# Router passes and Gelu's table moved among the last batches; up-products issued before the preceding down-products in the feed-forward stage

## Chip, cores and metric

One core of one Trainium2 chip runs the whole kernel. The metric is the device time of one execution in microseconds (us). Three executions of the kernel before took 1644.10, 1644.18 and 1648.24 us.

## The reference

16 sequences of 512 tokens with 128 features pass one layer. Cut to what matters for the change:

```python
h = take(W.T, x)                                     # 16 x 512 x 128
h = h + low_rank_attention(layernorm(h), W1, W2)     # one softmax over 512 keys
x = layernorm(h)
pooled = x.mean(axis=1)                              # 16 x 128
g = gelu(pooled @ router_w1.T + router_b1)
route = softmax(g @ router_w2.T + router_b2)         # 16 x 8
idx_s, idx_t = argmax(route[:, :4]), argmax(route[:, 4:])
fused = three_attentions(layernorm(x), idx_s, idx_t) # experts' weights by idx
x = x + fused
h2 = layernorm(x) * norm_mlp_w + norm_mlp_b
x = x + gelu(h2 @ mlp_w1.T + b1) @ mlp_w2.T + b2     # 128 -> 512 -> 128
out = h + x
```

The router (five lines from `pooled` on) needs the means of all 16 sequences. Its result says which experts' weights the attentions load.

## The kernel before

Three functions run one after the other, each in a block of its own. A block ends when every engine has come to the end of its program for it; the next one starts then. In a block each engine has its own program, in order, and semaphores join them. The helper `halves_of_pairs` calls a body for each batch number b, with the first pairs and the last ones written out and a hardware loop between them. A body handles several batches at different stages: `exists(b - 3)` is false where that batch is outside 0 to 15.

**embed_and_mix** gathers the tokens and does the first attention. Its second half has one step for each b:

- PE (`mix_and_turn`): the logits of b+1 (L620), the product of probabilities and X of b (`mix`, L632), then `turn` of b-3: 4 tokens' groups times a column of 1/512 into column b of a PSUM bank (L642, the pooling, 8 matmuls in the profile), and then the transposes of the twice normalised batch xh (L648). The two parts of `turn` stand in this order, and the first waits for `x_ready`, the second for `xh_ready`.
- ACT (`soften_and_keep`): Exp of b+1's logits (L526), `keep` of b-3 (L531 copies xs to X; L533 copies the transposed batch from PSUM to xhatT, after the transposes), `again` of b-2 (L541 writes xh, after DVE's `shift`).
- DVE (`second_norms`): the division and residual of b into h (L428, L432), its statistics, the shift of b-2 (L442), and normalise and statistics of b-1 (L356, L346, L351). POOL computes the reciprocal roots (L328, L332).

After the last step stands the router: DVE copies the pooled columns (L462), PE multiplies with router_w1 (L669), ACT applies Gelu (L556), PE multiplies with router_w2 (L671), DVE adds the bias and finds the maximum, ACT applies Exp with a sum (L558), DVE finishes softmax and argmax (L470 to L486), and SyncE stores the 32 numbers into the tile `expert` (L295). ACT keeps its functions in table sets. Where the program has no load of its own, the compiler sets one before the first function that needs another set: so before Gelu (L556), before the Exp behind it (L558) and in the block after (L1200).

**attend** is the long stage, 1270 us of the span. SyncE reads `expert` in it and loads w_in_S by it. The change leaves its code as it is.

**feed_forward** has one step for each b in each engine:

- PE (`stages`): `turn` of b (4 transposes, L1513; waits for `normed` and `hT_ready`), `down` of b-3 (32 matmuls in the profile, L1528; waits for the four Gelus of that batch), `up` of b-2 (8 matmuls, L1520; waits for hT, and for each quarter until the Gelu of the batch before it has read the PSUM bank).
- ACT (`gelu`): four Gelus for each batch (L1500), each as soon as its quarter of `up` is there. The tile gT has two halves, so Gelu of b waits until `down` of b-2 is done.
- DVE (`stages`): normalise of b (L1459), statistics of b+1, scale_shift of b-1 (hT, L1473; waits for `up` of b-3 to have read the tile's other use), `finish` of b-3 (y, L1467; waits for `down`, for POOL's base and for the store of y two batches back).
- POOL (`sequence`): the root of b, then base of b-4 (L1434, L1437), which waits for `finish` of the batch before, since `base` is one tile.
- SyncE fetches h of b+2 after base_a of b and stores y of b.

PE's step:

```python
if exists(b):
    turn(b, odd)
if exists(b - 3):
    down(b - 3, 1 - odd)
if exists(b - 2):
    up(b - 2, odd)
```

The batches' numbers in what follows are those of the argument, so turn(15) is the last batch's.

Of the kernel before, what the change touches and what calls it, by code (L numbers as in the profile page):

```python
# [6 lines left out]
ACT = mybir.ActivationFunctionType  # L7
# [7 lines left out]
B, T = 16, 512  # L15
NB = T // P
H, HD = 8, 16
K = 4
# [149 lines left out]
def tokens(tile, b, n):  # L168

    return tile[:, bass.ds(NB * b + n, 1), 0:P].rearrange("p o d -> p (o d)")  # L170


def embed_and_mix(nc, shared, x_ids, table, w12, router_w1, router_b1, router_w2, router_b2, norms, out_v):

    scrap, ident, low, high, eps_t, minus_half, norm_cols, expert, X, xhatT, psum = shared
    with ExitStack() as ctx:
# [91 lines left out]
        with nc.Block() as block:  # L268
# [74 lines left out]
            def _(dve):  # L343
# [79 lines left out]
                def second_norms(b, odd):  # L423

                    if exists(b):
                        dve.wait_ge(summed, b + 1)
                        sums = psum[:, 4:6, :].rearrange("p a (c e) -> p a c e", c=2)
                        nc.vector.reciprocal(rsum[:].rearrange("p (a c) -> p a c", a=2), sums[:, :, :, P])\  # L428
                            .then_inc(recip, 1)
                        dve.wait_ge(recip, b + 1)  # L430
                        for n in range(NB):
                            last = nc.vector.scalar_tensor_tensor(  # L432
                                out=tokens(h, b, n), in0=sums[:, n // 2, n % 2, 0:P], scalar=rsum[:, n:n + 1],
                                in1=tokens(h, b, n), op0=ALU.mult, op1=ALU.add)
                        last.then_inc(h2_ready, 1)
                        dve.wait_ge(h2_ready, b + 1)
                        settle(nc, scrap)
                        statistics(lambda n: tokens(h, b, n), b, six2, stats2, mv2[:, odd, :, :])
                    if exists(b - 2):
                        dve.wait_ge(rstd3, b - 1)  # L440
                        at_least(dve, xh_ready, b - 2)
                        nc.vector.scalar_tensor_tensor(out=shift3[:], in0=mv3[:, :, 0], scalar=-1.0, in1=rstd3_t[:],  # L442
                                                       op0=ALU.mult, op1=ALU.mult).then_inc(shift_ready, 1)
# [14 lines left out]
                halves_of_pairs(dve, second_norms, 2, B // 2, B // 2 + 1)  # L458


                dve.wait_ge(pooled_in, B)
                nc.vector.tensor_copy(pooled[:], psum[:, POOLED, 0:B]).then_inc(r_dve, 1)  # L462
                dve.wait_ge(r_pe, 2)
                nc.vector.tensor_tensor(rl[:], psum[0:B, 1, 0:2 * K], rb2[:], ALU.add).then_inc(r_dve, 1)
                dve.wait_ge(r_dve, 2)
# [23 lines left out]
            def _(act):  # L489
# [55 lines left out]
                def soften_and_keep(b, odd):  # L545
                    if exists(b + 1):
                        soften(b + 1, 1 - odd)
                    if exists(b - 3):
                        keep(b - 3, 1 - odd)
                    if exists(b - 2):  # L550
                        again(b - 2, odd)

                soften(0, 0)
                halves_of_pairs(act, soften_and_keep, 2, B // 2 - 1, B // 2 + 2)
                act.wait_ge(r_pe, 1)
                nc.scalar.activation(rh[:], psum[:, 0, 0:B], ACT.Gelu, bias=rb1[:]).then_inc(r_act, 1)  # L556
                act.wait_ge(r_dve, 4)
                nc.scalar.activation(rex[:], rl[:], ACT.Exp, bias=rsc[:, 1:2], accum_out=rsc[:, 2:3]).then_inc(r_act, 1)  # L558

            @block.tensor  # L560
            def _(pe):
# [74 lines left out]
                                start=(s == 0), stop=(s == NB - 1))  # L636
                    last.then_inc(summed, 1)

                def turn(b, odd):
                    pe.wait_ge(x_ready, b + 1)  # L640
                    for n in range(NB):
                        last = nc.tensor.matmul(psum[:, POOLED, bass.ds(b, 1)], xs[:, odd, n, :], mean_col[:],  # L642
                                                start=(n == 0), stop=(n == NB - 1))
                    last.then_inc(pooled_in, 1)
                    pe.wait_ge(xh_ready, b + 1)
                    at_least(pe, xhatT_kept, b)
                    for n in range(NB):
                        last = nc.tensor.transpose(psum[:, TURN, P * n:P * n + P], xh[:, n, :], ident[:])  # L648
                    last.then_inc(turned2, 1)

                def mix_and_turn(b, odd):
# [3 lines left out]
                        logits(b + 1)  # L655
                    if exists(b):
                        mix(b, odd)
                    if exists(b - 3):
                        turn(b - 3, 1 - odd)

                pe.wait_ge(rows_in[0], 16 * NPART)
                pe.wait_ge(x_kept[0], 8 * B)
# [1 line left out]
                pe.wait_ge(reduced, 2 * B)  # L664
                logits(0)
                halves_of_pairs(pe, mix_and_turn, 3, B // 2 - 1, B // 2 + 2)
                pe.wait_ge(r_dve, 1)
                pe.wait_ge(exped, B)
                nc.tensor.matmul(psum[:, 0, 0:B], rw1[:], pooled[:], start=True, stop=True).then_inc(r_pe, 1)  # L669
                pe.wait_ge(r_act, 1)  # L670
                nc.tensor.matmul(psum[0:B, 1, 0:2 * K], rh[:], rw2[:], start=True, stop=True).then_inc(r_pe, 1)  # L671


def attend(nc, shared, s_in, s_out, t_in, t_out, c_in, c_out, c_bias):
# [679 lines left out]
def feed_forward(nc, shared, mlp_w1, mlp_b1, mlp_w2, mlp_b2, out_v):  # L1354

    scrap, ident, low, high, eps_t, minus_half, norm_cols, expert, X, xhatT, psum = shared
    with ExitStack() as ctx:
# [31 lines left out]
        with nc.Block() as block:  # L1389
# [53 lines left out]
            def _(dve):  # L1443
# [32 lines left out]
                def stages(b, odd):  # L1476
# [3 lines left out]
                        statistics(b + 1)  # L1480
                    if exists(b - 1):
                        scale_shift(b - 1, 1 - odd)
                    if exists(b - 3):
                        finish(b - 3, 1 - odd)

                statistics(0)
                halves_of_pairs(dve, stages, 3, B // 2 - 1, B // 2 + 2)
# [18 lines left out]
            def _(pe):  # L1506
# [25 lines left out]
                def stages(b, odd):  # L1532
                    if exists(b):
                        turn(b, odd)
                    if exists(b - 3):
                        down(b - 3, 1 - odd)
                    if exists(b - 2):
                        up(b - 2, odd)

                halves_of_pairs(pe, stages, 3, B // 2, B // 2 + 2)  # L1540

# [59 lines left out]
```

## Time and profile before

| | |
|---|---|
| three executions | 1644.10, 1644.18, 1648.24 us (median 1644.18) |
| the profiled execution's own time | 1643.73 us |
| its span, first to last instruction | 1642.0 us |
| mean granted TensorE clock | 0.950 |
| PE busy | 1513.5 us, 92% of the span |
| DVE, ACT, POOL busy | 1221.4, 1129.2, 998.9 us |
| second half of embed_and_mix with the router | from 106.1 to 222.5 us |
| attend | from 222.5 to 1495.0 us |
| feed_forward | from 1495.0 us to the end |

The profile is of one execution. Times in it are microseconds from the first instruction, and 1643.73 - 1642.0 = 1.7 us lie around the span. A row of the timeline gives start, duration, engine, line, operation, tiles and count, and in square brackets how long the engine sat idle ahead of it and what ended that. PEld is TensorE's load of weights, which overlaps its matmuls. The ends of matmuls are modelled, so their starts are the better numbers. The granted clock is 1.00 at 2.4 GHz and 0.50 at 1.2 GHz.

### The profile page before, as it was taken

The numbers are of one execution on the slowest core, as the hardware profiler recorded it, in microseconds if no ns is written. First come the engines' busy times: TensorE is split into PE (matmuls) and PEld (weight loads), VectorE is DVE, ScalarE is ACT, GpSimd is POOL, SyncE is SP. The second block draws the span as 40 slices with busy tenths as digits, with TensorE's granted clock in tenths as the row PEclk, the third lists the DMA queues.
The fourth block names the chain that finished last, engine by engine and source line by source line (L and its number), as shares of the span: only waits on it lengthen the run. The fifth ranks groups of instructions, "written<-read, shape, count | busy, mean of one in ns | idle before, by whom it ended". The sixth has DMA issues, their size and how long they took to land. (4 is left out here: it accounts for less than half of the span.)

```text
span 1642.0 us, 37445 instructions
## 1 busy us (share of the span) xinstructions
PE 1513.5 (92%) x8694; PEld 662.1 (40%) x8694; DVE 1221.4 (74%) x3412; ACT 1129.2 (69%) x2201; POOL 998.9 (61%) x1359
## 2 busy tenths in 40 slices
PE   5779949899999999999999999999999999885998
PEld 1238823233333433333333333333333333212665
DVE  6868848489888887978888887978888897253442
ACT  5757733567887878787787878778787878723332
POOL 7704443756777776766777686776777684513443
PEclk9779957999999999999999999999999999957999
DMA  3311143644554654654564564564565552111221
GB/s 83 103 31 46 52 74 50 83 77 71 79 84 62 81 77 62 85 74 72 74 85 62 73 84 63 78 79 73 67 88 65 68 79 44 25 15 34 66 69 53
DMA packets 140020, 110.34 MB, mean 67 GB/s; under 512 B 22720, under 2 KB 134464, under 8 KB 139968
## 3 DMA queue, kind: packets, MB, share of 16 engines
q1 hardware_dynamic: 137920, 105.53, 43.4%
q0 software_dynamic: 2048, 4.20, 1.1%
q8 instruction: 23, 0.38, 0.1%
q14 instruction: 29, 0.24, 0.1%
HBM read 19.29 MB, written 8.39 MB: 17 GB/s over the span
## 5 line engine op out<-in xcount | busy, mean ns | idle before, releaser
L1153 ACT ACTIVATE probs<-psum 128x512 f32<-128x512 f32 (+3 forms) x1536 | 755.0, 548 | 225.7 <-PE psum L1268 215.0
L1053 DVE TENSOR_REDUCE mx_S<-psum 128x1 f32<-128x512 f32 x512 | 326.3, 681 | 48.6 <-PE psum L1248 47.6
L1053 DVE TENSOR_REDUCE mx_C<-psum 128x1 f32<-128x512 f32 x512 | 317.8, 676 | 45.3 <-PE psum L1248 45.3
L1049 DVE CUSTOM_DVE_ANT_0 psum<-psum,causal 128x128 f32<-128x128 f32 (+3 forms) x512 | 242.5, 509 | 98.1 <-PE psum L1248 95.5
L1248 PE MATMUL psum<-ks_S,qs_S 96*128 96x512 bf16 x512 | 197.6, 397 | 10.4 <-DMA ks_S<-parts_k 6.3
L1248 PE MATMUL psum<-ks_C,qs_C 96*128 96x512 bf16 x512 | 199.6, 398 | 4.6 <-DMA ks_C<-parts_k 1.4
L1268 PE MATMUL psum<-qs_C,ks_C 99*128 99x512 bf16 x512 | 189.3, 385 | 3.6 <-ACT probs L1153 3.2
L1268 PE MATMUL psum<-qs_S,ks_S 99*128 99x512 bf16 x512 | 190.5, 383 | 0.2
L934 POOL CAST parts_q<-f_q 128x512 bf16<-128x512 f32 x48 | 29.3, 610 | 226.7 <-ACT f_q L1144 226.2
L1248 PE MATMUL psum<-ks_T,qs_T 96*128 96x128 bf16 (+3 forms) x512 | 155.6, 306 | 1.6 <-DVE mx_S L1053 1.1
L1268 PE MATMUL psum<-qs_T,ks_T 99*128 99x256 bf16 (+3 forms) x512 | 152.1, 301 | 3.0 <-ACT probs L1153 1.7
L1287 PE MATMUL psum<-probs,va_S 128*32 128x512 f32 x1024 | 136.4, 604 | 1.6 <-ACT u_all L1173 0.3
L1287 PE MATMUL psum<-probs,va_C 128*32 128x512 f32 x1024 | 137.0, 607 | 0.8 <-ACT u_all L1173 0.6
L1248 PEld LDWEIGHTS psum<-ks_C,qs_C 96*128 96x128 bf16 x512 | 49.8, 97 | 166.8 <-DVE mx_C L1053 124.3
L922 POOL TENSOR_SCALAR_AFFINE_SELECT probs<-probs 128x512 f32<-128x512 f32 x128 | 81.0, 634 | 56.7 <-ACT probs L1153 53.7
L1248 PEld LDWEIGHTS psum<-ks_S,qs_S 96*128 96x128 bf16 x512 | 50.3, 99 | 153.9 <-DVE mx_S L1053 104.1
L1500 ACT ACTIVATE gT<-psum,b 128x512 f32<-128x512 f32 x64 | 44.0, 687 | 94.3 <-PE psum L1520 94.3
L1248 PEld LDWEIGHTS psum<-ks_T,qs_T 96*128 96x128 bf16 x512 | 50.1, 98 | 135.0 <-DVE mx_T L1049 91.2
L1287 PE MATMUL psum<-probs,va_T 128*32 128x512 f32 (+3 forms) x1024 | 96.3, 448 | 3.5 <-POOL probs L922 2.4
L988 POOL TENSOR_TENSOR s_all<-s_all,s_high 128x512 f32<-128x512 f32 x48 | 60.9, 1269 | 23.5 <-ACT u_high L1163 23.5
L316 POOL DMA_INDIRECT h<-in_table,ids x64 | 60.6, 947 | 20.4 <-issue 19.2
L1268 PEld LDWEIGHTS psum<-qs_C,ks_C 99*128 99x128 bf16 x512 | 49.4, 98 | 58.2 <-ACT probs L1153 23.9
(186 smaller groups left out, 2705.8 us busy)
## 6 DMA issues: line engine op xcount, KB each, us to landing
qs_S<-parts_q SPq DMA_DIRECT2D x96, 128.0 KB, 4.5
ks_S<-parts_k SPq DMA_DIRECT2D x96, 128.0 KB, 5.0
qs_T<-parts_q SPq DMA_DIRECT2D x96, 128.0 KB, 4.4
ks_T<-parts_k SPq DMA_DIRECT2D x96, 128.0 KB, 4.6
qs_C<-parts_q SPq DMA_DIRECT2D x96, 128.0 KB, 4.4
ks_C<-parts_k SPq DMA_DIRECT2D x96, 128.0 KB, 4.9
w_in_S<-in_s_in SPq DMA_DIRECT2D x16, 257.0 KB, 2.8
w_in_T<-in_t_in SPq DMA_DIRECT2D x16, 257.0 KB, 2.7
```

The source lines that it names most:

```text
L316: nc.gpsimd.indirect_dma_start(h[:, NB * b + n, :], None, table, bass.IndirectOffsetOnAxis(ap=ids[:, NB * b + n:NB * b + n + 1].bitcast(U3 ...
L922: nc.gpsimd.affine_select(out=diagonal, in_=diagonal, compare_op=ALU.is_ge, fill=0.0, base=0, pattern=[[0, 4], [1, P]], channel_multiplier ...
L934: nc.gpsimd.tensor_copy(parts[c][:, 0, :], f32[c][:]).then_inc(hi_done, 1)
L988: nc.gpsimd.tensor_tensor(s_all[:], s_all[:], s_high[:], ALU.add).then_inc(s_merged, 1)
L1049: nc.vector.tensor_tensor_reduce(tile[:, 0:last_key], tile[:, 0:last_key], causal[:, T - last_key:T], 1.0, NEG, ALU.add, ALU.max, mx[kind] ...
L1053: nc.vector.tensor_reduce(mx[kind][:, n:n + 1], tile, AX_X, ALU.max, negate=True).then_inc(reduced, 1)
L1153: nc.scalar.activation(probs[:, group_place(kind, b, n // 4), n % 4, t0:T], psum[:, LOGITS + ring_place(kind, b, n, RC), t0:T], ACT.Exp, s ...
L1248: nc.tensor.matmul(psum[:, ring_place(kind, b, n, RL), 0:keys], qs[kind][0:RA, hd, P * tb:P * tb + P], ks[kind][0:RA, hd, 0:keys], start=T ...
L1268: nc.tensor.matmul(psum[:, bank, t0:T], ks[kind][0:RB, hd, P * s:P * s + P], qs[kind][0:RB, hd, t0:T], start=True, stop=True).then_inc(log ...
L1287: last = nc.tensor.matmul(sums[32 * j:32 * j + 32, t0:T], va[kind][:, s, g, j, :], probs[:, group_place(kind, b, q), j, t0:T], start=(s == 0),
L1500: nc.scalar.activation(gT[:, odd, f, :], psum[:, 1 + f, :], ACT.Gelu, bias=b1[:, f:f + 1])\
```

## The change

In embed_and_mix:

- PE: the pooling is cut out of `turn` and called for b-2 ahead of `turn` of b-3. The router's two matmuls move from behind the last step into the last one with work (b = 18), between mix and turn(15).
- ACT: an explicit load of Gelu's table set stands in step 16, ahead of keep(13) and again(14). The router's Gelu and Exp stand in step 17 between keep(14) and again(15).
- DVE: the copy of the pooled columns moves into step 17, ahead of the shift of batch 15.

In feed_forward PE issues up of b-2 ahead of down of b-3, and DVE's `finish` comes one step later (b-4 in place of b-3).

```diff
@@ second_norms (DVE) @@
+                    if isinstance(b, int) and b == B + 1:
+                        dve.wait_ge(pooled_in, B)
+                        nc.vector.tensor_copy(pooled[:], psum[:, POOLED, 0:B]).then_inc(r_dve, 1)
                     if exists(b - 2):
                         dve.wait_ge(rstd3, b - 1)
...
-                dve.wait_ge(pooled_in, B)
-                nc.vector.tensor_copy(pooled[:], psum[:, POOLED, 0:B]).then_inc(r_dve, 1)
                 dve.wait_ge(r_pe, 2)
@@ soften_and_keep (ACT) @@
                     if exists(b + 1):
                         soften(b + 1, 1 - odd)
+                    if isinstance(b, int) and b == B:
+                        nc.scalar.add_instruction(mybir.InstLoadActFuncSet(
+                            name=nc.get_next_instruction_name(), engine=mybir.EngineType.Activation, ins=[], outs=[],
+                            act_func_set_id=GELU_SET))
                     if exists(b - 3):
                         keep(b - 3, 1 - odd)
+                    if isinstance(b, int) and b == B + 1:
+                        route()
                     if exists(b - 2):
                         again(b - 2, odd)
 
+                def route():
+                    act.wait_ge(r_pe, 1)
+                    nc.scalar.activation(rh[:], psum[:, 0, 0:B], ACT.Gelu, bias=rb1[:]).then_inc(r_act, 1)
+                    act.wait_ge(r_dve, 4)
+                    nc.scalar.activation(rex[:], rl[:], ACT.Exp, bias=rsc[:, 1:2], accum_out=rsc[:, 2:3]).then_inc(r_act, 1)
+
                 soften(0, 0)
                 halves_of_pairs(act, soften_and_keep, 2, B // 2 - 1, B // 2 + 2)
-                act.wait_ge(r_pe, 1)
-                nc.scalar.activation(rh[:], psum[:, 0, 0:B], ACT.Gelu, bias=rb1[:]).then_inc(r_act, 1)
-                act.wait_ge(r_dve, 4)
-                nc.scalar.activation(rex[:], rl[:], ACT.Exp, bias=rsc[:, 1:2], accum_out=rsc[:, 2:3]).then_inc(r_act, 1)
@@ PE @@
-                def turn(b, odd):
+                def pool_tokens(b, odd):
                     pe.wait_ge(x_ready, b + 1)
                     for n in range(NB):
                         last = nc.tensor.matmul(psum[:, POOLED, bass.ds(b, 1)], xs[:, odd, n, :], mean_col[:],
                                                 start=(n == 0), stop=(n == NB - 1))
                     last.then_inc(pooled_in, 1)
+
+                def turn(b, odd):
                     pe.wait_ge(xh_ready, b + 1)
...
                         mix(b, odd)
+                    if exists(b - 2):
+                        pool_tokens(b - 2, odd)
+                    if isinstance(b, int) and b == B + 2:
+                        route()
                     if exists(b - 3):
                         turn(b - 3, 1 - odd)
+
+                def route():
+                    pe.wait_ge(r_dve, 1)
+                    pe.wait_ge(exped, B)
+                    nc.tensor.matmul(psum[:, 0, 0:B], rw1[:], pooled[:], start=True, stop=True).then_inc(r_pe, 1)
+                    pe.wait_ge(r_act, 1)
+                    nc.tensor.matmul(psum[0:B, 1, 0:2 * K], rh[:], rw2[:], start=True, stop=True).then_inc(r_pe, 1)
...
-                pe.wait_ge(r_dve, 1)
-                pe.wait_ge(exped, B)
-                nc.tensor.matmul(psum[:, 0, 0:B], rw1[:], pooled[:], start=True, stop=True).then_inc(r_pe, 1)
-                pe.wait_ge(r_act, 1)
-                nc.tensor.matmul(psum[0:B, 1, 0:2 * K], rh[:], rw2[:], start=True, stop=True).then_inc(r_pe, 1)
@@ feed_forward, stages (DVE) @@
-                    if exists(b - 3):
-                        finish(b - 3, 1 - odd)
+                    if exists(b - 4):
+                        finish(b - 4, odd)
@@ feed_forward, stages (PE) @@
                         turn(b, odd)
+                    if exists(b - 2):
+                        up(b - 2, odd)
                     if exists(b - 3):
                         down(b - 3, 1 - odd)
-                    if exists(b - 2):
-                        up(b - 2, odd)
```

## Rows read from the trace of the kernel before

**Rows 1.** The page, part 4: shares of the span in the chain that ended last
```profile
PE psum L1528 4%; PE psum L1520 3%; ACT gT L1500 1%; DVE xs L1459 0%; PE psum L1513 0%; DVE y L1467 0%; DVE hT L1473 0%; DVE mv L1451 0%
```

**Rows 2.** Waits of PE, 1498 to 1642: total us, times, longest us
```profile
PE psum L1528 <- ACT gT L1500: 6.8, 15, 0.8
```

**Rows 3.** Timeline of the feed-forward stage, PE: one step in full
```profile
1513.49 3.84 PE L1528 MATMUL psum<-w,gT 128*128 128x128 f32 x32 [0.34 <-ACT gT L1500]
...
1517.17 3.60 PE L1520 MATMUL psum<-hT,w 128*128 128x512 f32 x8
...
1520.60 0.60 PE L1513 MATMUL psum<-ident,xs 128*128 128x128 f32 x4
...
1521.54 3.84 PE L1528 MATMUL psum<-w,gT 128*128 128x128 f32 x32 [0.34 <-ACT gT L1500]
```

**Rows 4.** Timeline of the feed-forward stage's last steps
```profile
1606.90 3.10 DVE L1459 TENSOR_SCALAR xs<-X,mv,rstd_t 128x128 f32<-128x128 f32 x4
...
1610.05 0.66 PE L1513 MATMUL psum<-ident,xs 128*128 128x128 f32 x4 [0.36 <-DVE xs L1459]
1610.54 3.77 PE L1528 MATMUL psum<-w,gT 128*128 128x128 f32 x32
1614.14 3.60 PE L1520 MATMUL psum<-hT,w 128*128 128x512 f32 x8
...
1618.52 3.84 PE L1528 MATMUL psum<-w,gT 128*128 128x128 f32 x32 [0.78 <-ACT gT L1500]
...
1630.45 0.69 DVE L1467 TENSOR_TENSOR y<-base,psum 128x512 f32<-128x512 f32 x1 [7.37 <-PE psum L1528]
...
1632.54 1.27 POOL L1437 TENSOR_TENSOR base<-base,b 128x512 f32<-128x512 f32 x1
```

**Rows 5.** Timeline of the end of embed_and_mix and of the router
```profile
208.22 1.11 DVE L356 TENSOR_SCALAR xs<-h,mv,rstd_t 128x128 f32<-128x128 f32 x4
208.23 1.65 ACT L541 ACTIVATE xh<-xs,shift,rstd 128x128 f32<-128x128 f32 x4 [0.92 <-DVE shift L442]
...
210.62 1.83 PEld L642 LDWEIGHTS psum<-mean_col,xs 128*128 128x128 f32 x8
...
212.25 1.65 ACT L541 ACTIVATE xh<-xs,shift,rstd 128x128 f32<-128x128 f32 x4 [0.57 <-DVE shift L442]
...
213.95 1.12 PE L648 MATMUL psum<-ident,xh 128*128 128x128 f32 x4 [1.40 <-ACT xh L541]
214.64 0.55 PEld L669 LDWEIGHTS psum<-pooled,rw 128*128 128x128 f32 x2
...
215.10 0.60 ACT L533 ACTIVATE xhatT<-psum 128x512 f32<-128x512 f32 x1 [0.69 <-PE psum L648]
215.72 1.28 ACT L556 ACT_TABLE_LOAD   x1
217.01 0.27 ACT L556 ACTIVATE rh<-psum,rb 128x16 f32<-128x16 f32 x1
...
218.80 0.18 ACT L558 ACTIVATION_READ_ACCUMULATOR rex<-rl,rsc 16x1 f32 x1
...
220.39 0.53 SPq L295 DMA_DIRECT2D expert<-rid_i  x1
222.52 1.28 ACT L1200 ACT_TABLE_LOAD   x1 [3.54 <-PEq L268]
```

**Rows 6.** Timeline at the end of attend and the block boundary behind it
```profile
1493.99 0.69 DVE L1120 TENSOR_TENSOR X<-X,psum 128x512 f32<-128x512 f32 x1 [4.98 <-PE psum L1304]
...
1494.97 1.28 ACT L1491 ACT_TABLE_LOAD   x1 [5.29 <-PEq L837]
```

**Rows 7.** Timeline of embed_and_mix, PE: mix(3), and a pooling in the loop
```profile
129.19 3.81 PE L632 MATMUL psum<-X,probs 128*128 128x129 f32 x32 [0.66 <-DVE h L432]
...
144.29 0.95 PE L642 MATMUL psum<-mean_col,xs 128*128 128x1 f32 x8
```

**Rows 8.** Busy time by stretch: us, PE, PEld, DVE, ACT, POOL, PEclk, DMA share, GB/s
```profile
275.00:309.00 34.00, 29.59 (x183) 9.88 (x181) 12.23 (x50) 28.47 (x60) 19.74 (x28) 1.00 0.41 56
```

## The prediction

> **What bounds the kernel now.** I read the page's chain of waits first. It ends in the feed-forward stage and goes through the down-products, the up-products and Gelu there [rows 1]. So that stage is bound by PE and by one wait on ACT. The waits of PE in the stage show it: 15 times PE sits idle ahead of the down-products until a Gelu is done, 6.8 us in all [rows 2]. The timeline of one step shows why. PE runs down, up, turn; the up-products' last quarter ends as turn begins, its Gelu ends after turn, and only then may the next down start [rows 3]. The up-products are thus directly ahead of the Gelu that the next down needs. In the last three steps there is no turn between them, and the idle time is 0.78 us instead of 0.34 [rows 4].
>
> The other edited place is the end of embed_and_mix. The timeline there is a serial chain: normalise, pooling, transposes, copy, table load, Gelu, Exp, the store of the experts' numbers, and then the next block [rows 5]. Nothing in that stretch has a bound; every engine waits most of the time. Attention between the two places has no edited code.
>
> **The feed-forward stage.** Nothing is added or removed; the order changes. The cost of a step, by starts, since the ends are modelled: down to up is 1517.17 - 1513.49 = 3.68 us; up to turn is 1520.60 - 1517.17 = 3.43 us; turn to down was 0.94 us [rows 3]. Without a wait for Gelu, turn to the next matmul takes 1610.54 - 1610.05 = 0.49 us: the one step in which turn itself came late shows that [rows 4]. A free step is 3.68 + 3.43 + 0.49 = 7.60 us. From the first down, 1513.49, to the thirteenth, 1610.54, there are 12 steps in 97.05 us [rows 3, 4], 8.09 us each. So a step with a turn loses 0.49 us, and there are 13: 6.4 us. The three steps without a turn: 1618.52 - 1614.14 = 4.38 us from up to down [rows 4] where 3.43 would do, 0.95 us each, 2.85 us in all. Sum 9.2 us.
>
> Does anything take the wait's place? With up of b-2 ahead of down of b-3, the down's Gelus were fed by the up-products of the step before, so they have a whole down of slack, 3.68 us. Gelu of b-2 needs down of b-4, which ends just ahead of this step's turn: no wait. The transposes need DVE's normalise. DVE now finishes b-4 at the start of PE's step b and normalises b+1 behind it (0.69 + 1.11 us), needed 7.6 us later; before, only up's 3.43 us lay between. That also covers the one slow normalise, 3.10 us at 1606.90 where others take 1.11, which made PE wait 0.36 us [rows 4, 5]. The queue of POOL: base of a batch waits for the finish of the batch before. At the very end down(15) now follows down(14) at once, in 3.7 to 3.8 us. From finish to the end of base it took 1632.54 + 1.27 - 1630.45 = 3.36 us [rows 4]. It fits with 0.4 us to spare; if it didn't, the excess would be late once. SyncE fetches h behind the same base and keeps a full step. Cost of all this: zero, with 1 us as the upper end, since PE's loop branches were covered by the wait for Gelu and could show. The lower end of the gain is the idle time alone, 6.8 + 0.36 = 7.2 us less that 1 us, 6.2; I take 9.2, because starts are recorded and ends are not.
>
> **The end of embed_and_mix.** Step by step, against the rows of before [rows 5].
> - Pooling one step earlier in the steady loop: the same work in each PE step. It needs x_ready, which DVE gives while PE is still in mix. In step 2 a pooling is now there that wasn't: 0.95 us against 0.66 us that PE then waited for DVE's h [rows 7]. It costs 0 to 0.3 us; I take 0, for starts in the loop put a pooling at 0.8 us and the idle time is short by as much.
> - The table load in step 16, 1.28 us, meets ACT's 0.92 us of idle time ahead of again(14). So again(14) starts at most 0.36 us late, 208.6, and ends at 210.2. It is hidden, since PE has the pooling to do first.
> - pool(15) no longer stands behind turn(14). x_ready comes at 208.22 + 1.11 = 209.33 and it loads from 209.4 in place of 210.62; at 1.8 us it is done at 211.2.
> - turn(14) follows at 211.2. From turn to the copy was 215.10 - 213.95 = 1.15 us, so xhatT of 14 is copied from 212.35 to 212.95. The router's first product loads 0.7 us after turn's start and takes 0.55 plus 0.1: 212.6.
> - Gelu follows the copy at once, 212.97, where it was at 217.01: 4.04 us sooner. What went: one batch's turn and copy, and 1.28 us of load.
> - From Gelu's start to the store of the experts' numbers was 220.39 - 217.01 = 3.38 us, and to the next block 5.51 us. By that branch alone the block would end at 218.5. Exp's own table load of 1.28 us stays in it.
> - The added wait: again(15) is queued behind Exp on ACT, and turn(15) and keep(15) behind it. Exp's sum is there 218.98 - 217.01 = 1.97 us after Gelu's start: again(15) at 214.95 instead of 212.25. From its start to the end of the last copy was 215.70 - 212.25 = 3.45 us, so ACT ends at 218.4.
> - The boundary of blocks: 0.3 us from the last instruction to the next block at the other boundary [rows 6], 2.1 us here from the store's issue, its landing included [rows 5]. I take 0.4, nearest to the first, since ACT's copy has no DMA behind it: 218.8. That is 222.5 - 218.8 = 3.7 us sooner, with 2.0 and 4.1 as the ends.
>
> ACT's load shows no drain: it lasts 1.28 us and Gelu starts 0.01 us behind it [rows 5]. The Trainium skill (ScalarE: Activation LUTs, What ACT_TABLE_LOAD costs) puts a drain of about 1.38 us on top of every load. By it the early load would push again(14) back by that much more; it is the third rival. The trace speaks against it.
>
> **The sum.** The profiled execution took 1643.73 us, 0.45 us under the median of 1644.18. 1643.73 - 9.2 - 3.7 = 1630.8 us, 0.8% less. A measurement of this kernel can tell about 0.3%, 5 us, from no change.
>
> **The rivals.**
> 1. *The feed-forward stage does not get faster* (6%). PE would find another wait in front of turn or up, as long as Gelu's was. For it: the stage has a single base tile and two halves of most others, and `finish` is one step later. Against: each slack worked out above is over 2 us, but for the last batch. Then 1643.73 - 3.7 = 1640.0.
> 2. *The router's branch gains nothing* (6%). That is so if the chain behind again(15) takes 3.7 us longer than worked out, or if the compiler sets its own loads around the explicit one, two more at 1.28 us each. For it: two chains end within 0.4 us of each other, so none has spare. Against: Copy and Identity run without a load behind Exp's set, and a load for Gelu of the program's own stands in front of the feed-forward stage without a second one. Then 1643.73 - 9.2 = 1634.5.
> 3. *Loads cost their drain* (2%). again(14) then starts 1.4 us later at 210.0, ends at 211.6, turn(14) and Gelu slip by 0.4, and another 1.4 us lies ahead of Exp and so of again(15): the block ends at 220.6. The time is 1643.73 - 9.2 - 1.9 = 1632.6. The page named above is where that drain stands.
> 4. *Slower: attention starts on a lower clock* (5%). The granted clock was 1.00 from 275 to 309, and PE was busy for 29.6 of these 34 us [rows 8]. Attention now begins 3.7 us earlier with regard to whatever sets the level, behind a stretch in which PE does little. If the whole of that stretch fell to 0.50, its matmuls would take up to 29.6 us more. This decides the sign from 12.9 us of matmul time at the lower level on. All of it gives 1660; two thirds give 1650, which I name as its time. For it: the level changed several times before 344 us, and three runs of one kernel spread over 4.1 us. Against: those runs have the same kind of start and differ by 4 us only. The Trainium skill (TensorE: Matmul & The Clock Gate, What's actually happening) says that the window in which activity is judged is free-running and does not begin with the kernel; the spread of the runs agrees with that and doesn't prove it.
>
> The forecast itself, both parts by these mechanisms, has the rest, 81%.
>
> **How the numbers follow.** The time is the forecast's, 1630.8. The ends of the known costs: feed-forward gains 6.2 to 9.5 us, the router 2.0 to 4.1, together 1630.1 to 1635.5. The clock moves it by some 4 us up as between the three runs and, as the start may also be luckier, as much down: 1626.1 to 1639.5. That takes in rivals 2 and 3 and leaves out rival 4 and rival 1, which are 11%. I keep 1626 to 1639. Faster by over 0.3% is under 1639.2: the forecast, rivals 2 and 3, 89%. Within 0.3% is rival 1 with a bit of the clock, 6%. Slower is rival 4, 5%.
>
> **What would show it.** In the changed profile: down-products start 7.6 us apart with no wait for Gelu ahead of them, and 7.1 us in the last steps; the waits of PE in the stage hold nothing for L1500's Gelu of note; down(15) directly follows down(14). In the router: one table load ahead of keep(13), none directly at Gelu, Gelu near 213.0, again(15) behind Exp near 215, the next block near 218.8, and ACT's last copy the later of the two ends. Wrong would be: idle time ahead of turn or up of 0.3 us or more in each step, a wait of DVE for POOL's base at the end, a second load in step 16 or 17, or a start of attention later than 220. The clock rival would show as longer matmuls between 222 and 344 at 0.50, with everything else as said.

## The result and the profile after

The changed kernel took 1628.04 us, the median of five executions (1627.90 to 1629.27). The kernel before, timed between them, took 1644.75 us (1644.10 to 1648.24). The ratio is 0.9899, with a 95% interval of 0.9885 to 0.9912. So the change made the kernel faster by 1.0%, 16.7 us by the medians. The forecast was 1630.8 us, in a range of 1626 to 1639.

The profiled execution took 1629.0 us and its span is 1627.2 us. Against before's 1643.73 and 1642.0 that is 14.7 and 14.8 us less. By stages, from one block's first table load to the next:

| | before | after | gained |
|---|---|---|---|
| up to the block behind the router | 222.52 us | 218.30 us | 4.2 us |
| attend | 1272.45 us | 1273.38 us | -0.9 us |
| feed_forward, table load to the last y's start | 143.53 us | 132.11 us | 11.4 us |

Of the first 4.2 us, 0.1 us lies ahead of the second half of embed_and_mix: its table load of Exp starts at 100.56 us before and at 100.44 us after. The last y of the kernel before, and in the changed kernel the table load that opens the last stage, POOL's last base and the last y (timelines):

```profile
1638.50 0.69 DVE L1467 TENSOR_TENSOR y<-base,psum 128x512 f32<-128x512 f32 x1 [7.37 <-PE psum L1528]
```

```profile
1491.68 1.28 ACT L1508 ACT_TABLE_LOAD   x1 [5.29 <-PEq L854]
...
1622.31 1.27 POOL L1454 TENSOR_TENSOR base<-base,b 128x512 f32<-128x512 f32 x1
1623.79 0.69 DVE L1484 TENSOR_TENSOR y<-base,psum 128x512 f32<-128x512 f32 x1 [2.89 <-PE psum L1545]
```

The page of the changed kernel, part 4, the chain that ended last:

```profile
PE psum L1545 4%; PE psum L1537 3%; PE psum L1530 0%; DVE xs L1476 0%; DVE hT L1490 0%; DVE y L1484 0%; DVE mv L1468 0%
```

Gelu, 1% of the chain before [rows 1], is no longer in it. Line numbers have moved by 17: the down-products are L1545, the up-products L1537, the transposes L1530. The busy time between the first and the last down-products of the changed kernel (columns: length, then busy us of PE, PEld, DVE, ACT, POOL, granted clock, DMA share, GB/s):

```profile
1513.00:1623.00 110.00, 110.00 (x668) 83.11 (x667) 65.03 (x169) 39.32 (x58) 50.54 (x52) 1.00 0.23 67
```

PE is busy for all of the 110 us. Its waits for a Gelu, 6.8 us in 15 times before [rows 2], are gone. The timeline of PE in the same kernel, one step and the last ones, answers to [rows 3, 4]:

```profile
1513.11 3.73 PE L1545 MATMUL psum<-w,gT 128*128 128x128 f32 x32
1516.68 0.60 PE L1530 MATMUL psum<-ident,xs 128*128 128x128 f32 x4
1517.12 3.60 PE L1537 MATMUL psum<-hT,w 128*128 128x512 f32 x8
1520.55 3.73 PE L1545 MATMUL psum<-w,gT 128*128 128x128 f32 x32
...
1609.43 3.73 PE L1545 MATMUL psum<-w,gT 128*128 128x128 f32 x32
...
1616.44 7.31 PE L1545 MATMUL psum<-w,gT 128*128 128x128 f32 x64
```

A step is 1520.55 - 1513.11 = 7.44 us, where 8.09 us was the mean before and 7.60 us the forecast. A last step, one without a turn, is 1616.44 - 1609.43 = 7.01 us. The last two down-products are one row of 64 matmuls: nothing lies between them.

The end of embed_and_mix in the changed kernel, from the timeline (answers to [rows 5]):

```profile
205.96 1.28 ACT L550 ACT_TABLE_LOAD   x1
...
207.25 0.63 ACT L532 ACTIVATE X<-xs 128x512 f32<-128x512 f32 x1
...
211.08 1.09 PE L659 MATMUL psum<-ident,xh 128*128 128x128 f32 x4
211.26 0.17 DVE L441 COPY pooled<-psum 128x16 f32<-128x16 f32 x1 [0.63 <-PE psum L651]
...
212.22 0.60 ACT L534 ACTIVATE xhatT<-psum 128x512 f32<-128x512 f32 x1 [1.79 <-PE psum L659]
212.71 0.27 ACT L562 ACTIVATE rh<-psum,rb 128x16 f32<-128x16 f32 x1
213.00 1.28 ACT L564 ACT_TABLE_LOAD   x1
...
214.59 1.63 ACT L542 ACTIVATE xh<-xs,shift,rstd 128x128 f32<-128x128 f32 x4
...
216.08 0.53 SPq L295 DMA_DIRECT2D expert<-rid_i  x1
...
217.43 0.60 ACT L534 ACTIVATE xhatT<-psum 128x512 f32<-128x512 f32 x1 [0.69 <-PE psum L659]
218.30 1.28 ACT L1217 ACT_TABLE_LOAD   x1 [0.28 <-PEq L268]
```

Every step stands in the order that was worked out. There is one load of Gelu's set, at 205.96, and the copy behind it starts 0.01 us after its end. Gelu runs at 212.71 instead of 217.01. again(15), at 214.59, now stands behind Exp, and ACT's last copy ends at 218.03. The next block begins 0.3 us later. The store of the experts' numbers, issued at 216.08, had 2.22 us by then; before, the block began 2.13 us after its issue. So the two branches end almost together: by before's 2.13 us the store alone would let the block begin at 218.21, 0.1 us sooner than it did. (The load that opens the block, L1217 here and L1200 before, is the program's own and not the compiler's.)

### The profile page after: what moved, and what is told of

Read it like the earlier page. It is cut to its first block and busy times, and to the rows that moved or that the text cites. A ratio compares the mean times of both kernels' runs of the same rounds, so it can differ in the third digit from the quotient of the medians.

```text
span 1627.2 us, 37445 instructions
## 1 busy us (share of the span) xinstructions
PE 1510.4 (93%) x8694; PEld 661.2 (41%) x8694; DVE 1241.3 (76%) x3412; ACT 1129.1 (69%) x2201; POOL 1000.1 (61%) x1359
```

## The experiments

These ran on three other chips of the same kind, on which the kernel before takes 1704 to 1705 us. The surplus lies in the first stage: the load of Exp's table ahead of the second half starts at 159.35 us in the changed kernel on the third of them and at 100.44 us on the chip above. From there on its stages last as long as here: 118.0 us to the next block (117.9 here), 1273.5 us of attention (1273.4), and 132.1 us of feed-forward (132.1). Each kernel is compared with the kernel before on its own chip, and stages are compared by traces. Times on the timeline in the expectations are those of the first chip, so some 59 us have to be added.

**The two parts alone.** The first kernel has embed_and_mix of the changed kernel and feed_forward of before, the second the other way round.

> The edits of embed_and_mix alone, feed_forward as before. Theory A (the two parts do not touch each other): the block after the router starts at 218.3 us as in the changed kernel, the stage of feed_forward lasts 144.2 us from its table load to its last y as before, and the time is 4.2 us under the kernel before, give or take 1 us in attention. Theory B (the shift of attention's start against the clock levels made part of the gain): attention lasts more than 2 us less or more than before's 1272.5 us, and the time is off by as much.

> The edits of feed_forward alone, embed_and_mix as before. Theory A (the two parts add): the stage lasts 132.8 us in place of 144.2, down-products start 7.44 us apart, and the time is 11.4 us under the kernel before. Theory of the prediction as it stood: 9.2 us, with 7.60 us from down to down.

The router's part alone: 1700.32 us against 1703.85, ratio 0.9978 (0.9968 to 0.9987), 3.5 us less. The feed-forward part alone: 1693.07 us, ratio 0.9944 (0.9928 to 0.9960), 10.8 us less. The changed kernel itself was timed again on a third chip:

> The changed kernel itself, timed on the same chip as the kernel with up ahead of turn. It serves as the mark for that kernel: the stage of feed_forward should last 131.8 us from its table load to its last down-product's start, and the time be 15 to 17 us under the kernel before.

1687.82 us against 1703.83, ratio 0.9904 (0.9887 to 0.9920), 16.0 us less; 3.5 + 10.8 = 14.3 us is within the runs' spread of that. In the traces the feed-forward stage shows the parts cleanly. The first fence is the timeline of the router's part alone, the second that of the feed-forward part alone (in each the table load that opens the stage, and the last y).

```profile
1554.02 1.28 ACT L1508 ACT_TABLE_LOAD   x1 [5.29 <-PEq L854]
...
1698.23 0.69 DVE L1484 TENSOR_TENSOR y<-base,psum 128x512 f32<-128x512 f32 x1 [7.37 <-PE psum L1545]
```

```profile
1554.09 1.28 ACT L1491 ACT_TABLE_LOAD   x1 [5.31 <-PEq L837]
...
1686.33 0.69 DVE L1467 TENSOR_TENSOR y<-base,psum 128x512 f32<-128x512 f32 x1 [2.88 <-PE psum L1528]
```

144.2 us and 132.2 us, with 7.44 us from down to down in the second (starts at 1590.54 and 1597.98); the whole change has 132.1 us. The first is 0.7 us longer than the 143.5 us of before; the expectations' 144.2 and 132.8 us counted to the end of the last y, and by that measure these are 144.9 and 132.9 us. The 0.7 us lie in the first up-products: 5.79 us to the transposes behind them instead of 5.13, at a granted clock of 0.59 instead of 0.66. At the end of embed_and_mix, Gelu's table load to the next block is 12.35 us in the router's part alone and 12.34 us in the changed kernel. So theory A holds for the two edited stages.

Theory B, of attention, is not excluded. Its mark was met in the first kernel: attention lasts 1275.95 us there, 3.5 us more than the 1272.45 us of before. The router's part as such does not bring that much, for the changed kernel has the same embed_and_mix and 1273.4 and 1273.5 us in two traces. But in the nine traces with the router moved attention lasts 1270.6 to 1276.0 us, 0.7 us more on average than in the four with the router in its old place, 1272.2 to 1272.5 us. The section on the prediction comes back to it.

**Why a step is 7.44 and not 7.60 us.** In the kernel before, down waits for three of the four Gelus and takes the third quarter twice in place of the fourth, so it leaves out a part of the result. PE's order is that of before.

```diff
-                    pe.wait_ge(gelu_done, F // P * b + F // P)
+                    pe.wait_ge(gelu_done, F // P * b + F // P - 1)
...
-                            last = nc.tensor.matmul(psum[:, DOWN[odd], P * n:P * n + P], gT[:, odd, f, P * n:P * n + P],
+                            last = nc.tensor.matmul(psum[:, DOWN[odd], P * n:P * n + P], gT[:, odd, min(f, 2), P * n:P * n + P],
```

> The kernel before, where down waits for three of its four Gelus and multiplies the third quarter of gT twice in place of the fourth (PE's work is the same in size; the fourth Gelu runs and nobody reads it). PE's order is that of before. Theory A (the loss of before was the wait for Gelu and, with it, the first load of weights, which a waiting matmul cannot have ahead of time: 0.11 us at down and 0.05 at turn): steps with a turn are 7.44 us apart, as in the changed kernel, and only the last three keep a short wait of 0.1 us or less; the stage lasts 133 to 134 us and the time is 10 to 11 us under the kernel before. Theory B (the order itself is cheaper, down to turn than down to up): 7.60 us a step, and 8 to 9 us under the kernel before.

1692.69 us against 1703.85, ratio 0.9934 (0.9919 to 0.9950), 11.2 us less. The timeline of PE in that kernel:

```profile
1580.95 3.74 PE L1528 MATMUL psum<-w,gT 128*128 128x128 f32 x32
1584.53 3.60 PE L1520 MATMUL psum<-hT,w 128*128 128x512 f32 x8
1587.96 0.60 PE L1513 MATMUL psum<-ident,xs 128*128 128x128 f32 x4
1588.40 3.74 PE L1528 MATMUL psum<-w,gT 128*128 128x128 f32 x32
```

Down, up, turn as before, and 7.45 us a step: theory A. In the steps of the loop the order is worth nothing by itself; the wait was all of it. The whole stage is 133.3 us to the last y's start, 1.1 us longer than with the changed order on the same chip: PE still waits 0.36 us for the one late normalise (of 3.10 us), and the last steps take 7.19 us instead of 7.01. And the wait cost more than its idle time: a step of 8.05 us, 0.34 us of it idle, became one of 7.44. Weight loads (PEld) show what. First the kernel before, the load and the matmul of a down that waited, then the changed kernel, where the first load runs ahead of its matmul and 31 are left in the row behind:

```profile
1618.52 3.65 PEld L1528 LDWEIGHTS psum<-w,gT 128*128 128x128 f32 x32 [1.61 <-ACT gT L1500]
```

```profile
1520.12 0.19 PEld L1545 LDWEIGHTS psum<-w,gT 128*128 128x128 f32 x1 [0.24 <-issue]
1520.55 3.54 PEld L1545 LDWEIGHTS psum<-w,gT 128*128 128x128 f32 x31 [0.24 <-issue]
```

Before, the load started with its matmul, at 1618.52 [rows 4]. Now it is done 0.24 us before the matmul starts, under the up-products. Down to the next kind takes 3.57 us instead of 3.68, and turn to the next 0.44 instead of 0.49. That it is the load that costs this is read from these rows; no run changed the load alone.

**The Gelu table.** The changed kernel without the explicit load.

```diff
-                    if isinstance(b, int) and b == B:
-                        nc.scalar.add_instruction(mybir.InstLoadActFuncSet(
-                            name=nc.get_next_instruction_name(), engine=mybir.EngineType.Activation, ins=[], outs=[],
-                            act_func_set_id=GELU_SET))
```

> The changed kernel without the explicit load of Gelu's table set in step 16; the compiler then sets one directly ahead of Gelu. Theory A (ACT's chain of Gelu, Exp, again(15) and keep(15) ends the block): Gelu starts at 214.0 instead of 212.7 and the next block at 219.6 instead of 218.3, 1.3 us later. Theory B (something else ends the block, and ACT has spare time): the next block starts less than 0.5 us later.

1688.26 us against 1704.96, ratio 0.9903 (0.9887 to 0.9920). In time that can't be told from the changed kernel (0.9904). The timeline of this kernel can tell it:

```profile
270.75 0.17 DVE L441 COPY pooled<-psum 128x16 f32<-128x16 f32 x1 [0.63 <-PE psum L647]
...
272.32 1.28 ACT L558 ACT_TABLE_LOAD   x1
273.62 0.27 ACT L558 ACTIVATE rh<-psum,rb 128x16 f32<-128x16 f32 x1
...
279.21 1.28 ACT L1213 ACT_TABLE_LOAD   x1 [0.28 <-PEq L268]
```

From the pooled copy to the next block it takes 279.21 - 270.75 = 8.46 us. In the changed kernel it is 218.30 - 211.26 = 7.04 us. The early load is worth 1.4 us of the router's 4.2, and of the two theories A holds: what hangs on ACT's Gelu ends the block. It does not tell ACT's own end from the store of the experts' numbers, for both moved with Gelu. The store is issued 2.22 us ahead of the next block here too, and ACT's last copy ends 0.27 us ahead of it. That ACT's is the later end, by some 0.1 us, rests on the 2.13 us of before.

**The pooling alone.** The kernel before, with the pooling moved ahead as in the change and nothing else.

```diff
+                    if exists(b - 2):
+                        pool_tokens(b - 2, odd)
                     if exists(b - 3):
                         turn(b - 3, 1 - odd)
```

> The kernel before, with the pooling of b-2 ahead of turn of b-3 and nothing else: the router stays behind the last step and its table loads stay where they were. Theory A (the gain comes from the router's place on ACT and PE, and the early pooling only allows it): the pooled copy comes some 1.3 us sooner, Gelu and the next block come when they did, within 0.2 us, and the time is that of the kernel before. Theory B (the pooling was on the chain): 1.3 us sooner.

1703.85 us in a single execution; the median of before on that chip is 1703.83. From its timeline:

```profile
271.91 0.17 DVE L462 COPY pooled<-psum 128x16 f32<-128x16 f32 x1
...
272.51 1.63 ACT L541 ACTIVATE xh<-xs,shift,rstd 128x128 f32<-128x128 f32 x4
...
282.77 1.28 ACT L1204 ACT_TABLE_LOAD   x1 [3.53 <-PEq L268]
```

From again(15) to the next block it is 10.26 us, and 222.52 - 212.25 = 10.27 us before [rows 5]. The pooled copy is 10.86 us ahead of the block instead of 9.94, 0.9 us sooner rather than 1.3, since in DVE's program it still stands behind the shift of batch 15, and nobody uses it. Theory A holds: the early pooling only makes room for the router's place.

**The slow normalise.** In the changed kernel DVE's normalise takes 3.06 to 3.10 us for the last eleven of the 16 batches and 2.35 us for the one ahead of them, where it took 1.11 us before and 3.10 us once [rows 4]. Its timeline:

```profile
1583.87 0.69 DVE L1484 TENSOR_TENSOR y<-base,psum 128x512 f32<-128x512 f32 x1 [1.72 <-PE psum L1545]
...
1584.47 3.07 DVE L1476 TENSOR_SCALAR xs<-X,mv,rstd_t 128x128 f32<-128x128 f32 x4
...
1584.81 1.30 POOL L1451 TENSOR_TENSOR base<-h,X 128x512 f32<-128x512 f32 x1 [1.98 <-DVE y L1484]
```

Both wait for the same y: POOL's base starts beside the normalise. The experiment cuts POOL's two adds to one column of each token group, with base set to zero once.

```diff
-                        nc.gpsimd.tensor_tensor(base[:], h2[:, odd, :, :], X[:, bass.ds(NB * c, NB), 0:P], ALU.add)\
+                        nc.gpsimd.tensor_tensor(base[:, :, 0:1], h2[:, odd, :, 0:1], X[:, bass.ds(NB * c, NB), 0:1], ALU.add)\
```

> The changed kernel, where POOL adds one column of each token group into base in place of 128 (the rest of base is set to zero once), so that its two adds are near 0.2 us each in place of 1.3. Theory A (DVE's normalise takes 3.07 us in place of 1.11 because POOL's adds of base run beside it): it takes 1.1 us in all steps, and the stage is as long as in the changed kernel, 132.8 us, since PE waits for neither. Theory B (the long normalise comes from something in DVE's own program, like the loop's branch or the fetch of code): it stays at 3.07 us.

From the timeline of that kernel:

```profile
1583.45 1.11 DVE L1479 TENSOR_SCALAR xs<-X,mv,rstd_t 128x128 f32 x4
1583.79 0.32 POOL L1454 TENSOR_TENSOR base<-h,X 128x4 f32<-128x4 f32 x1 [4.11 <-DVE y L1487]
```

1.11 us in every step, so theory A holds. The one slow normalise of before fits it: POOL's base starts at 1607.12 there, beside it, and beside none of the others. The step stays at 7.44 us and the stage at 132.2 us: PE does not wait for either. The single execution took 1687.53 us.

**The later finish.** The changed kernel with DVE's finish left at b-3, and the same with POOL's adds cut.

```diff
-                    if exists(b - 4):
-                        finish(b - 4, odd)
+                    if exists(b - 3):
+                        finish(b - 3, 1 - odd)
```

> The changed kernel, with DVE's finish left at b-3 in its step as before; PE's order is the changed one. DVE then normalises the next batch only after a down that ends PE's step. Theory A (the later finish is what hides DVE; POOL's base runs beside that normalise): PE waits ahead of each turn for y and a normalise of 3.07 us, 0.65 + 3.1 us, some 3.7 us in each of 13 steps, and the time is 35 to 50 us over the changed kernel, so over 20 us slower than the kernel before. Theory B (the normalise is not slowed there): 1.8 us a step, 20 to 25 us over the changed kernel.

> The kernel with finish left at b-3 and with POOL's adds into base cut to one column of each token group. Theory A (POOL's adds slow the normalise that PE waits for): the wait ahead of each turn falls from 3.7 to 1.8 us, and the time is 25 us under that of the kernel with the whole adds. Theory B: both take the same time.

The first took 1724.10 us against 1704.96, ratio 1.0119 (1.0102 to 1.0136), 19.1 us over the kernel before. Its feed-forward stage lasts 168.1 us to the last y's start, 36.0 us over the changed kernel's. Its waits of PE in the stage from 1562 us on (total, times, longest), and its timeline in the loop and at the last transposes:

```profile
PE psum L1530 <- DVE xs L1476: 28.5, 13, 3.8
```

```profile
1578.63 1.02 POOL L1444 TENSOR_TENSOR rstd_t<-vare,minus_half 128x4 f32<-128x4 f32 x1
1579.62 1.18 POOL L1451 TENSOR_TENSOR base<-h,X 128x512 f32<-128x512 f32 x1
...
1586.60 0.66 PE L1530 MATMUL psum<-ident,xs 128*128 128x128 f32 x4 [1.81 <-DVE xs L1476]
...
1687.26 3.08 DVE L1476 TENSOR_SCALAR xs<-X,mv,rstd_t 128x128 f32<-128x128 f32 x4
...
1690.39 1.12 PE L1530 MATMUL psum<-ident,xs 128*128 128x128 f32 x4 [3.78 <-DVE xs L1476]
```

The total over the changed kernel is where theory A had it, but not for its reason. In the loop PE waits 1.81 to 2.27 us for a normalise of 1.11 us, nearly as theory B had it; only the last wait is 3.78 us. These twelve waits are 25.9 us. The row's thirteenth, 2.66 us, is at the start of the stage, and the changed kernel has it too. POOL's base is in the loop not beside the normalise (that of this step starts at 1575.96, base at 1579.62), because POOL's queue has the root of the next batch ahead of it, and that needs statistics which DVE computes after the normalise. Without roots in the last step, base starts at once.

Of the other 10.1 us, 7.5 us are the granted clock. The row of busy time for one of the slow steps of that kernel:

```profile
1590.50:1601.80 11.30, 9.41 (x46) 6.17 (x45) 3.57 (x15) 2.81 (x5) 4.78 (x5) 0.85 0.22 63
```

PE had been idle for 1.9 us ahead of the transposes. The clock was on the lower level for a part of the stretch, the up-products took 5.13 us to the next kind instead of 3.44, and the step took 11.24 us where its neighbours took 9.47 and 9.63. There are four such steps, the last behind the wait of 3.78 us; in up-products and transposes they lose 1.7, 1.5, 1.7 and 2.6 us. The last 2.6 us are 0.2 us in each of the twelve steps: from down to the transposes it is 5.54 us with a wait of 1.81, where 3.57 + 1.81 = 5.38, and 0.49 instead of 0.44 us behind them.

With POOL's adds cut the single execution took 1721.01 us, and its stage 163.6 us, 4.4 us less than with the whole adds. The waits of the loop are the same to 0.01 us. The difference comes from the step of the last transposes:

```profile
1690.50 0.66 PE L1533 MATMUL psum<-ident,xs 128*128 128x128 f32 x4 [1.81 <-DVE xs L1479]
```

The wait is 2.0 us shorter there, with a normalise of 1.11 us instead of 3.08, and the transposes and up-products behind it, at the full clock, save 2.6 us more. So theory A's 25 us did not come: the normalise runs beside base only at that one place. What was not run is the other half, DVE's later finish with PE's order of before.

**A kernel with up ahead of turn.** In the changed kernel the first up-products wait behind turn(2), though their input is there. The step is reordered again.

```diff
                 def stages(b, odd):
-                    if exists(b):
-                        turn(b, odd)
                     if exists(b - 2):
                         up(b - 2, odd)
+                    if exists(b):
+                        turn(b, odd)
                     if exists(b - 3):
                         down(b - 3, 1 - odd)
```

> The changed kernel, with PE's step in feed_forward as up of b-2, turn of b, down of b-3. Theory (turn's place in the step costs nothing in the steady steps, but in step 2 the first up-products wait behind turn(2), whose normalise ends at 1503.2 while hT of batch 0 is there at 1501.3): down-products stay 7.44 us apart, the first up starts at 1501.3 instead of 1504.1, and the time is 2 to 3 us under the changed kernel, some 18.5 us under the kernel before. Rival (the start goes by DVE and POOL, or the granted clock is at its lower level for longer): less than 1 us.

> The changed kernel, with PE's step in feed_forward as up of b-2, turn of b, down of b-3, beside the changed kernel on the same chip. Theory: 2.5 us less in the stage, 129.3 us, and 2 to 3 us less in the time; rival: attention or the clock gives it back, and both kernels take the same time within 1 us.

First 1687.56 us against 1703.85, ratio 0.9908 (0.9893 to 0.9922), 16.3 us less where the theory had 18.5. Then, beside the changed kernel, 1687.10 us (1684.88 to 1689.91) against its 1687.82 us (1686.00 to 1689.14), with ratios 0.9905 (0.9888 to 0.9921) and 0.9904. The traces of that second pair, first the changed kernel and then up first, PE's row of the first up-products and DVE's of the last y:

```profile
1563.31 5.27 PE L1537 MATMUL psum<-hT,w 128*128 128x512 f32 x8
...
1682.96 0.69 DVE L1484 TENSOR_TENSOR y<-base,psum 128x512 f32<-128x512 f32 x1 [2.88 <-PE psum L1545]
```

```profile
1560.56 5.24 PE L1537 MATMUL psum<-hT,w 128*128 128x512 f32 x8 [0.78 <-DVE hT L1490]
...
1680.65 0.69 DVE L1484 TENSOR_TENSOR y<-base,psum 128x512 f32<-128x512 f32 x1 [2.89 <-PE psum L1545]
```

Both stages open at 1550.9 us. Up starts 2.75 us sooner and the last y is 2.3 us sooner, 129.8 us after the stage's first load instead of 132.1. So the stage is shorter as the theory said, but executions of one kernel spread over 3 to 7 us here, and the medians, 0.7 us apart, do not show it. Whether the whole kernel gains these 2.3 us is left open.

## Why the prediction was right

The mechanism of both parts was right, and the time lies in the range, 2.8 us under the forecast. But both terms came out at or beyond their own upper ends: feed-forward gained 11.4 us where the ends were 6.2 and 9.5, of which the 9.5 is worked out from no row, and the router 4.1 to 4.2 us where they were 2.0 and 4.1. By those ends alone the time would have been 1630.1 to 1635.5 us. The gain is 16.7 us by the medians where 12.9 had been worked out. The time lies within 1626 to 1639 because 4 us had been allowed to either side for the clock, and it was the terms that used them; that much is luck. Without the 0.9 us that attention gave back it would have been 1627.1. The steps one by one:

- *Feed-forward, 9.2 us.* It was 11.4 us. The step that was mis-sized is the free step of 3.68 + 3.43 + 0.49 = 7.60 us. Its 3.68 and 0.49 came from matmuls that had waited, the first for Gelu and the second for a late normalise, and so had their first weights loaded after the wait. Free, they take 3.57 and 0.44 us, 0.16 us less a step. 13 steps give 2.1 us, and the last ones, 7.01 instead of 7.11, give the rest. The prediction's own rows held a better value: the down at 1610.54 had not waited, and up starts 1614.14 - 1610.54 = 3.60 us after it [rows 4]. The kernel with the short wait showed that this belongs, in the loop, to the wait and not to the order.
- *Nothing takes the wait's place.* Right, and with room to spare but at the end. Leaving finish at b-3 turned the gain of 1.0% into a loss of 1.2%, so this part of the change needs the later finish as much as the new order. The prediction had named it, as the step that gives the normalise 7.6 us, but had put no price on its absence.
- *The slow normalise.* The prediction took the 3.10 us as a single case that would be covered. It became the rule, with 3.07 us from the sixth batch on, and was covered all the same. Its cause, POOL's base beside it, had not been seen. The prediction's slack for DVE, 7.6 us, was wide enough to hold it.
- *The end.* base was ready at 1623.58, 0.2 us ahead of the last y, which started as its down ended. 0.4 us had been worked out, with 3.7 to 3.8 us for that down; it took 3.58, by the starts of the last two y.
- *The router, 3.7 us.* It was 4.2 us. Gelu came at 212.71, not 212.97. The copy ahead of it started 0.13 us sooner, and Gelu starts 0.11 us before that copy ends, while with a table load between them it starts 0.01 us (before) and 0.02 us (without the early load) behind the load. The block's boundary took 0.3 us, not 0.4. The 0.3 us that step 2's pooling might have cost came to 0.1 us at most: mix(3) starts 28.73 us behind Exp's table load instead of 28.63.
- *again(15) behind Exp.* It was put at 214.95 and came at 214.59, and the copy behind it ends the block, by 0.1 us over the store's branch, as worked out.
- *Attention.* It was 0.9 us longer in the profiled execution. No term stood for it but the range.

Of the rivals, the first, that feed-forward gains nothing, fell with the rows above, and so did the second, that the router's branch gains nothing: there is one explicit load, and none follows it ahead of Gelu. The third, a drain of 1.4 us on a table load, did not show in either place: X's copy starts 0.01 us after the load at 205.96, and Gelu 0.02 us after the load at 272.32 in the kernel without the early one. The fourth, attention on a lower clock, did not come as a loss of many us, but something of it shows. The granted clock of its first stretch was 0.72 against 0.77 before, in the rows of busy time of the changed kernel and of the kernel before:

```profile
218.30:340.00 121.70, 97.97 (x397) 36.75 (x398) 78.25 (x183) 45.83 (x92) 67.25 (x92) 0.72 0.57 80
```

```profile
222.50:344.00 121.50, 95.11 (x405) 37.17 (x409) 79.39 (x185) 46.96 (x94) 66.85 (x91) 0.77 0.55 79
```

PE was busy 2.9 us longer in nearly the same time, with eight matmuls fewer. The loss falls early: the sixth load of w_in_S is issued at 524.17 us before, 301.65 us behind the start of the block, and at 521.20 us in the changed kernel, 302.90 us behind it. From there on the issues are 73.4 us apart in both, so more than the 0.9 us arises ahead of that point.

The 13 traces say a little more. In the stretch from 40 to 122 us behind the start of the block the granted clock was 0.84 to 0.86 in the four kernels with the router in its old place and in two traces of the nine others, and attention lasts 1270.6 to 1272.5 us in these six. It was 0.77 to 0.81 in the other seven, and attention lasts 1272.8 to 1276.0 us. So the surplus goes with the clock of that stretch. Whether the earlier start of attention brings the lower clock is not shown: in two of the nine it did not.

## What to carry to other kernels

In a loop bound by one engine that hands each batch to another and takes it back, put the work that feeds the other engine ahead of the work that needs its answer, and move the consumers' order along with it: here the second edit, DVE's finish one step later, decided between a gain of 1.0% and a loss of 1.2% for the whole change. When a wait on PE is costed, take the length of the free matmuls from groups that did not wait themselves; a group that waited shows its first weight load, too. Before a vector operation is moved, ask what POOL will run beside it.

## What was not expected of the hardware

DVE's normalise of 128x128 f32, four instructions, takes 1.11 us alone and 3.07 us beside POOL's adds of 128x512 f32, while the first of POOL's adds takes 1.18 to 1.30 us beside it instead of 1.18. In the kernel with finish kept, PE waits 1.8 to 2.3 us in each step of 9.5 to 9.9 us of the loop. In three of these steps the granted clock was on its lower level for a time, which cost 1.5 to 1.7 us each, and a fourth time behind the wait of 3.78 us, which cost 2.6 us. With the waits of 0.34 to 0.78 us before, and with none after, it stayed at 1.00 from the first down-products to the last.
